# Attention walks of a four-layer graph network: masks fetched four blocks at a time from a table laid out by partition

## The reference, cut to what matters

```python
w = jnp.einsum('ehd,ehd->eh', q[e_dst], k[e_src])
mx = jax.ops.segment_max(w, e_dst, num_segments=n)
ex = jnp.exp(w - mx[e_dst])
den = jax.ops.segment_sum(ex, e_dst, num_segments=n)
```

## Time and profile before

| | us |
|---|---|
| median of 3 runs | 6143.33 (6137.6 to 6145.03) |
| span of the profiled execution | 7315.2 |
| layer 0's edge walk (L1129, L974), with the mask table's store | about 215 to 1540 |
| walk `l1te`, first mask load to last step | about 1572 to 2990 |
| walk `l3te` | about 5850 to 7315 |

### The profile page before, as it was taken

One profiled execution on the slowest core, in us unless ns is written; L12 is line 12 of the kernel. 1 busy time (PEld: TensorE's weight loads), 2 busy tenths in 40 slices (PEclk: granted clock), 3 DMA queues, 4 the chain that ended last, 5 costly groups with the idle time before them and its releaser, 6 DMA issues. The chain is left out here.

```text
span 7315.2 us, 90173 instructions
## 1 busy us (share of the span) xinstructions
PE 4476.1 (61%) x19030; PEld 3617.6 (49%) x19030; DVE 4054.5 (55%) x11905; ACT 1218.9 (17%) x3505; POOL 4097.0 (56%) x4195
## 2 busy tenths in 40 slices
PE   4577777746666666786666666444434446667666
PEld 4466666635555555443444444233333335556555
DVE  7344444436666666754555555344444446666665
ACT  4122222211111111251111111000000111111111
POOL 1565655645555655104666666566666556566563
PEclk9866666666666666798888888655555566666665
DMA  2433333323333333345444444212212333333333
GB/s 48 127 90 94 93 95 93 92 87 100 104 103 104 107 105 105 72 181 196 134 131 132 135 130 129 59 57 58 58 58 58 52 109 113 108 116 109 109 114 65
DMA packets 451977, 737.64 MB, mean 101 GB/s; under 512 B 103370, under 2 KB 309283, under 8 KB 444996
## 3 DMA queue, kind: packets, MB, share of 16 engines
q0 software_dynamic: 173296, 436.67, 21.8%
q1 hardware_dynamic: 269684, 289.63, 12.1%
q10 hardware_dynamic: 8592, 6.82, 0.4%
HBM read 613.74 MB, written 120.20 MB: 100 GB/s over the span
## 5 line engine op out<-in xcount | busy, mean ns | idle before, releaser
L1564 POOL DMA_INDIRECT xh<-pair_d,src_i x1658 | 1646.1, 993 | 1196.2 <-issue 447.5
L2390 POOL DMA_INDIRECT l2e_rows<-msg_d,msg_i x829 | 807.0, 973 | 619.4 <-issue 209.1
L974 POOL DMA_INDIRECT l0e_rows<-node_d,src_i x832 | 792.1, 952 | 535.6 <-PE l0e_ps L1130 294.4
L1129 PE MATMUL l0e_ps<-l0e_rows,l0e_sel 128*128 128x256 f32 x1664 | 806.3, 582 | 385.0 <-issue 186.8
L829 POOL DMA_INDIRECT l2f_rows<-msg_d,msg_i x829 | 785.5, 948 | 428.8 <-issue 229.6
L863 PE MATMUL l2f_ps<-l2f_rows,l2f_sel 128*128 128x128 f32 x1664 | 418.7, 421 | 594.7 <-DVE xh L894 351.3
L2503 PE MATMUL l2e_ps<-l2e_rows,l2e_sel 128*128 128x256 f32 x1664 | 484.1, 423 | 421.0 <-DVE l2e_sel L2595 403.9
L863 PEld LDWEIGHTS l2f_ps<-l2f_rows,l2f_sel 128*128 128x128 f32 x1664 | 372.3, 314 | 670.8 <-issue 405.9
L1194 DVE TENSOR_TENSOR early_acc<-early_acc,l0e_ps 128x264 f32 x832 | 356.8, 429 | 544.4 <-issue 234.4
L2562 DVE TENSOR_TENSOR l_acc<-l_acc,l2e_ps 128x256 f32 x832 | 349.5, 420 | 509.0 <-DMA l0e_rows<-node_d,src_i 332.5
L894 DVE TENSOR_TENSOR xh<-xh,l2f_ps 128x128 f32 x832 | 238.6, 287 | 675.7 <-DMA l2e_rows<-msg_d,msg_i 460.8
(11 more groups left out here) (443 smaller groups left out, 7961.9 us busy)
## 6 DMA issues: line engine op xcount, KB each, us to landing
l0e_rows<-in_edge_attr_dram SPq DMA_DIRECT2D x832, 64.0 KB
msg_d<-l2a_msg SPq DMA_DIRECT2D x50, 1024.0 KB
l1te_local<-local_d SPq DMA_DIRECT2D x52, 512.0 KB
l2e_local<-local_d SPq DMA_DIRECT2D x52, 512.0 KB
l3te_local<-local_d SPq DMA_DIRECT2D x52, 512.0 KB
xh<-pair_d,src_i POOLq DMA_INDIRECT x1658
msg_d<-l2e_msg SPq DMA_DIRECT2D x50, 512.0 KB
l0e_rows<-node_d,src_i POOLq DMA_INDIRECT x832
```

The costliest lines, as they stand in the source:

```text
L974: pool.indirect_dma_start(rows[:, t % R, 0:D], None, table, bass.IndirectOffsetOnAxis(g.src_i[:, t:t + 1], 0)).then_inc(gathered[t % R], 16)
L1129: nc.tensor.matmul(ps[r % B][:, 0:2 * D], sel[:, r // G % 2, r % G, :], rows[:, r, :], start=True, stop=True)
L1564: pool.indirect_dma_start(rows[:, t % R, :], None, g.pair_d, bass.IndirectOffsetOnAxis(g.src_i[:, t:t + 1], 0)).then_inc(gathered[n % RG], 16)
L2390: pool.indirect_dma_start(rows[:, t % R, :], None, table, bass.IndirectOffsetOnAxis(index[:, t:t + 1], 0)).then_inc(gathered[t % R], 16)
```

## The change

The table becomes `mask_d[head and tile of the block (128), block (52) x 1 KB]`: a row for each partition of the block's square, so that four blocks' masks lie side by side in a row of it as 4 KB. `store_masks` writes it with 52 DMAs, one per block, each from 16 partitions of `g.mask`, eight copies of 1 KB. In the walks `load_masks` fetches four blocks' masks (128 rows of 4 KB, 512 KB) and ends at once, 13 times, into two buffers of four blocks; it stands behind `local` of blocks 0, 2, 6, 10 ... and waits for `fell` of the group before the last. `over` moves onto unused rows of `g.coef`, `mf` and half of `weights` are left out in `l3te`, which makes room.

```diff
@@ store_masks
-    for b in range(TB):
-        n = min(P, T - b * P)
-        act.dma_start(view(g.mask_d.tensor, b * P * HS * 4 * P, [[HS * 4 * P, n], [4 * P, HS], [1, 4 * P]]),
-                      g.mask[0:n, b, :, :].rearrange("p k e -> p (k e)").unsqueeze(1)
-                      .broadcast_to([n, HS, 4 * P])).then_inc(g.masks_out, 16)
+    for s in range(NS):
+        b, p0 = s * S // P, s * S % P
+        act.dma_start(view(g.mask_d.tensor, s * 4 * P, [[HS * NS * 4 * P, S], [NS * 4 * P, HS], [1, 4 * P]]),
+                      g.mask[p0:p0 + S, b, :, :].rearrange("p k e -> p (k e)").unsqueeze(1)
+                      .broadcast_to([S, HS, 4 * P])).then_inc(g.masks_out, 16)
@@ attention_edges
+    M = 4
-        mask = st.sb("mask", [P, 2, 4, P], BF16)
-        ends = st.sb("ends", [HS, 2, 2, S])
+        masks = st.sb("mask", [P, 2, M, 4, P], BF16)
+        ends = st.sb("ends", [HS, 2, 2, M * S])
-        over = st.sb("over", [HS, T + 1])
+        over = g.coef[0:HS, 0:T + 1]
-        mf = st.sb("mf", [P, P])
-        weights = st.sb("weights", [P, 2, 2, S, HS])
+        mf = st.sb("mf", [P, P]) if first else None
+        weights = st.sb("weights", [P, 2, 2 if first else 1, S, HS])
@@ SyncE
+                def load_masks(j):
+                    if j >= 2:
+                        sp.wait_ge(fell, M * (j - 1))
+                        if first:
+                            sp.wait_ge(firsts, M * (j - 1))
+                    sp.dma_start(masks[:, j % 2, :, :, :].rearrange("p s k e -> p (s k e)"),
+                                 g.mask_d[:, j * M * 4 * P:(j + 1) * M * 4 * P]).then_inc(mask_in[j % 2], 16)
+                    sp.dma_start(ends[:, j % 2, :, :], view(g.ends_d.tensor, j * M * S, [[0, HS], [TA, 2], [1, M * S]])) \
+                        .then_inc(mask_in[j % 2], 16)
-                    if s >= 2:
-                        sp.wait_ge(fell, s - 1)
-                        if first:
-                            sp.wait_ge(firsts, s - 1)
-                    sp.dma_start(mask[:, b, :, :].rearrange("p k e -> p (k e)"), g.mask_d[s * P:(s + 1) * P, :]) \
-                        .then_inc(mask_in[b], 16)
-                    sp.dma_start(ends[:, b, :, :], view(g.ends_d.tensor, s * S, [[0, HS], [TA, 2], [1, S]])) \
-                        .then_inc(mask_in[b], 16)
+                    if s == 0:
+                        load_masks(0)
+                    if s % M == 2 and s // M + 1 < NS // M:
+                        load_masks(s // M + 1)
@@ scan_forward (the other readers of the masks change in the same way)
-                    dve.wait_ge(mask_in[b % 2], 32 * (b // 2 + 1))
+                    dve.wait_ge(mask_in[b // M % 2], 32 * (b // M // 2 + 1))
@@ gnn_stack
-        g.mask_d = nc.dram_tensor("mask_d", (T * HS, 4 * P), BF16, kind="Internal").ap()
+        g.mask_d = nc.dram_tensor("mask_d", (P, NS * 4 * P), BF16, kind="Internal").ap()
```

More of the change, by code:

```diff
@@ L1030, in _ @@
                     sp.wait_ge(one, 16 * NW)
[L1031 removed]
+                sp.wait_ge(g.masks_out, 16 * (NS + 2))
             @block.scalar
@@ L1552, in attention_edges, with mask_of @@
                 "diagd", "exturn", "alspread", "factored", "scaled", "weighted", "beside", "summed", "added", "taken"))
+        def mask_of(b, k):
+            return masks[:, b // M % 2, b % M, k, :]
         def slot(t):
@@ L1824, in scan_forward @@
                     dve.wait_ge(scores_turned, b + 1)
-                    dve.wait_ge(mask_in[b % 2], 32 * (b // 2 + 1))
+                    dve.wait_ge(mask_in[b // M % 2], 32 * (b // M // 2 + 1))
                     if b >= 1:
                         dve.wait_ge(joined, 2 * b)
-                    nc.vector.tensor_tensor_scan(both[:, 0:P], mask[:, b % 2, 0, :], pb[:, 0:P], FAR,
+                    nc.vector.tensor_tensor_scan(both[:, 0:P], mask_of(b, 0), pb[:, 0:P], FAR,
                                                  ALU.add, ALU.max).then_inc(scanned, 1)
                 def scan_back(b):
-                    nc.vector.tensor_tensor_scan(both[:, 2 * P - 1:P - 1:-1], mask[:, b % 2, 1, ::-1], pb[:, P - 1::-1], FAR,
+                    nc.vector.tensor_tensor_scan(both[:, 2 * P - 1:P - 1:-1], masks[:, b // M % 2, b % M, 1, ::-1], pb[:, P - 1::-1], FAR,
                                                  ALU.add, ALU.max).then_inc(scanned, 1)
@@ L1847, in scan_carries @@
                         dve.wait_ge(handed, b)
-                    nc.vector.tensor_tensor_scan(over[:, b * S + 1:(b + 1) * S + 1], ends[:, b % 2, 0, :], pb[0:HS, P:P + S],
+                    nc.vector.tensor_tensor_scan(over[:, b * S + 1:(b + 1) * S + 1], ends[:, b // M % 2, 0, b % M * S:(b % M + 1) * S], pb[0:HS, P:P + S],
                                                  over[:, b * S:b * S + 1], ALU.add, ALU.max).then_inc(carried, 1)
-                    nc.vector.tensor_tensor_scan(back[:, S - 2::-1], ends[:, b % 2, 1, S - 1:0:-1],
+                    nc.vector.tensor_tensor_scan(back[:, S - 2::-1], ends[:, b // M % 2, 1, b % M * S + S - 1:b % M * S:-1],
                                                  pb[0:HS, P + 2 * S - 1:P + S:-1], FAR, ALU.add, ALU.max).then_inc(carried, 1)
@@ L1870, in join_ends @@
                     for k in range(2):
-                        nc.vector.scalar_tensor_tensor(join[:, k, :], mask[:, b % 2, 2 + k, :], carry[:, k:k + 1],
+                        nc.vector.scalar_tensor_tensor(join[:, k, :], mask_of(b, 2 + k), carry[:, k:k + 1],
                                                        both[:, k * P:(k + 1) * P], ALU.add, ALU.max).then_inc(joined, 1)
@@ L1889, in shift @@
                             dve.wait_ge(ex_turned, b)
-                    nc.vector.scalar_tensor_tensor(fall[:, :], mask[0:HS, b % 2, 2, 0:1], over[:, b * S:b * S + 1],
+                    nc.vector.scalar_tensor_tensor(fall[:, :], masks[0:HS, b // M % 2, b % M, 2, 0:1], over[:, b * S:b * S + 1],
                                                    top[0:HS, 0:1], ALU.add, ALU.subtract).then_inc(fell, 1)
@@ L1893, in shift @@
                     if first:
-                        nc.vector.scalar_tensor_tensor(mf[:, :], mask[:, b % 2, 0, :], -1.0, top[:, :],
+                        nc.vector.scalar_tensor_tensor(mf[:, :], mask_of(b, 0), -1.0, top[:, :],
                                                        ALU.is_lt, ALU.mult).then_inc(firsts, 1)
```

## The result

The changed kernel takes 6147.91 us (median of 20 runs, 6137.0 to 6156.72) against 6134.73 us of the kernel before in 20 runs beside it (6122.94 to 6145.79): ratio 1.002, 95% interval 1.0013 to 1.0027. It is slower by 13 us. Forecast were +7 us and 6150.

A forecast was written before the change was run, and what follows sets the result against it. No engine or bandwidth was full; the VectorE, TensorE and GpSimd chain paced the walks, and the store stood on the path. Walk starts +2 and store +5 gave +7 us on 6143.33, so 6150, range 6130 to 6190.

The forecast's parts named there:

- The masks were never late: In both walks, the scan L1828 idles for TensorE's scores_turned, not for mask loads, so loading masks earlier gains 0.
- The reading of 32.0 us between issue and use: In l1te, a mask load is issued 32.0 us before its block's scan, so it can hardly be late.
- Rival B: In the walks, scans do wait for masks: up to 246 us faster, 5897; chance 0.12 with smaller gains of its kind.
- SyncE's wait and its shorter queue: In the walks, fewer waits for fell and 28 us less of SyncE's queue a walk are worth 0.
- What bounds a walk: In both walks, the VectorE, TensorE and GpSimd chain sets the pace; GpSimd idles mostly for VectorE's L1922.
- Start of each walk, +2: At each walk's start, 768 KB more masks load beside the first gathers: +1 us a walk, +2 for both.
- The store, +5: The table store on ScalarE's queue, with 52 small DMAs in 25 to 31 us, delays TensorE's next work by 5 us.
- rival A: The store gets only four paths out of SBUF, 96 GB/s: +32 us, 6177; chance 0.38 including the ground towards the forecast.
- The queue's own limit: On ScalarE's queue, issuing 52 store DMAs at 0.36 us each takes 19 us, at best 6 us less than now.
- rival D: The walks gain nothing and the store is limited by its issues: -6 + 2, 6139; chance 0.10.
- The sharing of paths out of SBUF: In the store, 16 neighbouring partitions may reach only four paths, 96 GB/s; two DMAs in flight reach eight, 193 GB/s.
- a quarter of the moving go on behind ScalarE's back: At the store's end, ScalarE is free while the last quarter still moves, so at 274 with eight paths: +5 us.

The follow-up runs named there:

- experiment 3: The changed kernel with its new table written by 7 DMAs from 128 partitions, against the kernel before: 1.0056, 7393.90 us; store 40.84 us.
- experiment 1: The kernel before, unchanged, profiled again on a slower chip: 7349.08 us; its store of 7 DMAs took 22.35 us.
- experiment 2: The new walks (four blocks a load) on the old table and 7-DMA store, against the kernel before: 1.0037, 7373.26 us.
- experiment 6: The changed kernel with its 52 store DMAs handed out between layer 0's conversions, up to four at a time, against the kernel before: 6105.42 us, 0.9957.
- experiment 7: The kernel before with its 7 store DMAs handed out one at a time between layer 0's conversions, against the kernel before: 6110.1 us, 0.9971.
- experiment 10: The kernel before with 52 store DMAs, each of 16 partitions mostly lying 8 apart; only the store's time is read: 37.59 us.
- experiment 4: The kernel before with only its store changed, to 52 DMAs of 16 neighbouring partitions into the old table: 1.0025, 7362.96 us; store 43.71 us.
- experiment 5: The changed kernel run again, unaltered, on a quicker chip against the kernel before: 1.0015; store 43.90 us.
- experiment 9: The kernel before, unchanged, profiled once more on a slower chip (before 7464.57 us there): store 24.36 us.
- experiment 12: The new walks on the old table, its 7 store DMAs handed out one at a time, against the kernel before: 0.9949, 7433.33 us.

## Why the prediction was right, and where it was off

*The masks were never late.* Right, and shown: on the quicker chip L1828 and its successor wait 0.1 us in `l1te` in either layout. The reading of 32.0 us between issue and use was the sound one, and the release by "DMA" a name of a semaphore used twice. On the slower chips the scans do wait, but not for masks. In the stretch shown above ScalarE's L1744, which needs TensorE's result and no mask, goes on 0.12 us ahead of the scan. And in experiment 3, with a group's masks issued 124 us ahead, the scan waits 7.91 us as before:

```profile
2846.62 0.32 SPq L1579 DMA_DIRECT2D l1te_mask<-mask_d  x1
2970.23 0.42 DVE L1839 TENSOR_TENSOR_SCAN l1te_both<-l1te_mask,l1te_pb 128x128 f32<-128x128 bf16 x1 [7.91 <-DMA tb_raw<-edges_d,starti]
```

What is put down to "DMA" there even grew, from 125.8 us in experiment 1 to 200.8 in experiment 2 and 239.1 in experiment 3. Rival B falls on both kinds.

*SyncE's wait and its shorter queue:* 0, right on the quicker chip; the walks of experiments 6 and 7 are equal within what traces of one walk differ by. On the first slower chip it stays open, see the end.

*What bounds a walk.* I took GpSimd to stand idle mostly for VectorE. That was so in the slower chip's trace alone. On the quicker one GpSimd's gathers are the pace (1042 us busy and issuing), which makes the walks still less sensitive to a mask load.

*Start of each walk, +2:* not found. `l3te` waits 3.4 to 4.4 us for its first `local` with the new loads and 2.6 to 3.8 with the old ones on the quicker chip; the two ranges overlap.

*The store, +5.* This is the term that was mis-sized. Place and mechanism were right (ScalarE's queue, microsecond for microsecond into TensorE's wait), the size was 19.0 us (43.70 against 24.72) and TensorE's wait grew by as much (38.81 against 19.84). In the prediction's own terms that is no longer the forecast's store (25 to 31 us) but lies in the ground between it and rival A. Two sub-steps failed:

1. The queue's own limit, "52 x 0.36 = 19 us". The 0.36 us were read on SyncE, with a DMA of another shape. On ScalarE such a DMA in a row of them takes at least 0.61 us (607 ns in experiment 10), and with the step to the next (37.59 / 52) 0.72 us on average. From 24.36 us for 7 DMAs to 37.59 for 52 whose partitions are spread: 13 us for the count and the size of the DMAs. The mechanism is rival D's, a store limited by its issues, with its price turned from -6 to +13.
2. The sharing of paths out of SBUF. It exists but is the smaller part: 6 us (experiment 10 against 4). Rival A, four paths at 96 GB/s, would have had the moving at 71 us; it does not hold, the steady rate was 174 GB/s. Nor is that the 193 of eight paths of 24.1 GB/s. It is no fixed limit either: in the burst from 234 to 238 the store's queue alone moved 343 GB/s (its packets in the trace, summed), out of the same DMAs of 16 neighbours, which had piled up beside the other transfers, as I read it. How many paths there are was measured by no run, and experiment 10 was limited by the queue, so what the neighbours cost without that limit is not known. The port rule of the Trainium skill ("SBUF — State Buffer", "Door 1: The DMA port swizzle") gives 104 GB/s for one transfer from partitions 0 to 15; a row of DMAs, each from the next 16 partitions, moved more here, 174 GB/s. The direction agrees, the loss of some 28 us that I estimated from it does not: it was 19.

I also let a quarter of the moving go on behind ScalarE's back. With small DMAs there is no such backlog at the end: ScalarE is free at 262.10, and from 262 to 266 the DMA share is 0.45 already.

*Sum.* 19 us on the path and 11 to 13 us in the time. That a microsecond more here moves the end by the same was my premise, and it did not quite hold: layer 0 can make a part of the stall good behind it. Busy time in the same stretch after the store, in the changed kernel's first trace and in experiment 5:

```profile
270.00:280.00 10.00, 10.00 (x61) 9.12 (x61) 6.72 (x19) 1.97 (x3) 7.56 (x9) 1.00 0.49 133
```
```profile
270.00:280.00 10.00, 10.00 (x33) 8.60 (x32) 4.11 (x12) 1.31 (x2) 7.30 (x9) 1.00 0.39 106
```

The kernel is the same and TensorE is busy throughout, but it does 61 matmuls in the one and 33 in the other; a pair of L1129 takes 0.68 us there and 1.20 here, at a granted clock of 1.00 (2.4 GHz) in both. The first had layer 0's conversions done in 1102.9 us, the second in 1116.3, and their times are 6137.0 and 6148.55 us. So whether some 12 us come back is settled within 40 us after the store, and it differs between two executions; what settles it is open, and so is how often it happens.

*Luck.* That 6147.91 lies 2 us from the 6150 is luck: the 6143.33 that I started from, a median of three runs, was 9 us above the 6134.73 of 20. The change itself was +13 against +7, just beyond the 0 to +12 that I had given 0.37.

In favour of the new walks there is only that experiment 6 beats 7 by 4.7 us with overlapping intervals, while their walks are equally long in the traces. That is open.

*Open as well:* on the first slower chip (experiments 1 to 4) both kernels with the new walks lost time that their stores do not explain, 20 and 26 us, and `l1te` took 1386.0 and 1392.7 us in them against 1358.9 and 1363.8 with the old walks. On the second slower chip (9 to 12) the same walk code was no longer than the old one (first to last `selt` 1399.1 us in experiment 12, in the slowest of its six runs, against 1402.5 in experiment 9). So the new walks may cost 20 to 26 us on one chip and nothing on two others. Late masks are not the reason, as shown above; no run shows what is.

## What to carry to other kernels

Ask of every DMA that is moved or cut up which engine's queue issues it and what stands behind it there: the loads that this change made larger had been hidden all along, and the store that it cut into 52 pieces stood in front of TensorE's next work. Take the price of an issue from a row of the same queue and shape. And a store that nobody waits for until the end of a stage is best handed out between the queue's other work: that was worth 18 us to the old kernel and 33 to the new one.

## What was not expected of the hardware

- One and the same kernel took 6128 to 6135 us on some chips and 7350 to 7465 us on others. Most of it lies in stretches of over 3 us in which TensorE, VectorE and ScalarE all stand: 944 us against 25. 51 steps of `l1te` take 1037.1 us on the quicker chip and 1358.9 on the slower.
- In rows of DMAs, once the burst at their start is over, 32 neighbouring partitions in one DMA moved 244 GB/s, 16 neighbours 174 (and 343 within the burst), and 16 that lie 8 apart 199, where the queue was the limit; DMAs of 128 partitions moved 380.
- After the store, the same kernel's TensorE did 61 matmuls in 10 us in one run and 33 in another, at a granted clock of 1.00 in both.
- A destination whose outermost dimension is 8 kept the DMA share at 0.56 and took 40.84 us for what 16 engines moved in 24.
